# A decoder layer with a mixture-of-experts feed-forward: six experts' output products with tokens as columns, later GpSimd low parts, last norm on VectorE

## The chip, the cores and the metric

The kernel runs on one core of one Trainium2 chip. The metric is the device time of one execution in microseconds. A core has TensorE (PE; its weight loads are PEld), VectorE (DVE), ScalarE (ACT), GpSimd (POOL) and SyncE (SP), which here only issues DMAs. Each engine works through its own instructions in order; between engines the order is kept by semaphores alone. TensorE's clock has two levels here, 1.2 and 2.4 GHz, of which the chip grants one.

## The reference, cut to what matters

`x` is 16 x 512 x 256, in f32. One layer follows: an attention with its norm, a cross-attention with its norm, and the part that the change touches, a feed-forward of eight experts with a last norm:

```python
routing_weights = softmax(x @ router_w.T + router_b)            # tokens x 8
routing_mask = (w_flat > 0)
sorted_indices = argsort(-routing_mask, stable=True)[:capacity] # capacity = 1024 as the kernel uses it
inter = relu(einsum('ceh,ehi->cei', inputs_tokens, experts_inter))   # 256 -> 1024
out = einsum('cei,eih->ceh', inter, experts_out)                     # 1024 -> 256
out = out * inputs_weights[..., None]
combined = zeros_like(x_flat).at[used_tokens_indices].add(out)
x = layernorm(x + combined)
```

Every expert takes the first 1,024 tokens whose weight for it is above zero. When all weights are above zero, all eight experts take the same first 1,024 tokens, and all other rows only get the norm.

## The kernel before

`setup_and_attention` computes both attentions, tile by tile of 128 tokens, writes `x2` (the input of the feed-forward) to DRAM, and also writes the normed rows of all tokens to the output. `feed_forward` then handles groups of `CAP` = 1,024 tokens. After each group the number of groups is read from a register; with these inputs one group runs. Its accumulator `acc` holds the group's tokens, eight tiles (`GT`) of 128 tokens as partitions and 256 columns.

All matrix products run as `three_passes` (L134 to L139): each operand is kept as a high part in f32r and a low part (the rest), and TensorE adds high x high, low x high (or high x low) and the third combination into one PSUM bank, so one block of a product costs three matmuls.

For each expert (`expert(g, n, e, u)` in each engine's program; `u` is the one of two weight buffers in use):

- *First product* (`pe_tile`, L1576): for both halves `h` of 512 tokens and 8 chunks `i` of hidden columns, 6 matmuls with 512 columns (tokens) in one of four `up` banks. ScalarE writes the ReLU's high part `hT_hi` (L1489), VectorE the low part `hT_lo` and frees the bank (L1742). Hidden units lie on partitions, tokens are columns.
- *Output product* (L1655 to L1665): for each of 8 token tiles, 24 matmuls whose weights are 128 tokens of `hT` and whose 256 columns are the output channels of `w2`, in one of two `dn` banks. VectorE multiplies by the routing coefficient of the tokens (a column per partition) and adds into `acc` (L1755), which frees the bank.
- *Next weights*: SyncE loads `w1_raw` and `w2_raw` (one buffer each, 1 MB each, L86 and L87) once the low parts of the expert before are made. ScalarE makes the high parts (L1454, L1457) in four pieces at `i % 4 == 3` of the first product, GpSimd the low parts, one instruction of 128 x 2048 for each (L1518).

Expert 0 also makes the routing: logits, softmax, `chosen` (weight above zero), `ranks` by matmuls after the first output tile (L1664), and then on VectorE `coefficients` (L1725): steps 6 to 9 make `coef`, steps 10 to 12 the number of groups. The first six of expert 0's first products run in the last slots of the attention.

After each tile of expert 7 VectorE makes the statistics (L1760, L1762). For each pair of tiles GpSimd makes the scale and offset in four small instructions (L1542 to L1548), ScalarE applies them (L1509), and SyncE stores the pair (L1432).

## Time and profile before

| | us |
|---|---|
| median of 3 runs (lowest, highest) | 1288.14 (1287.87, 1289.94) |
| the profiled execution, its own time | 1288.03 |
| its span, first to last instruction | 1286.1 |
| TensorE busy | 1242.2 (97%) |
| VectorE busy | 876.0 (68%) |
| GpSimd busy | 632.1 (49%) |
| ScalarE busy | 574.5 (45%) |

The feed-forward takes about the last quarter of the span, from some 920 us on. Times in the rows are in microseconds from the span's start unless they are marked ns. A busy share is a mean over stages with different limits, so a stage has to be read by itself. TensorE's matmuls are pipelined, and their ends in the profile are modelled: the distance from start to start is what one costs. In a row in order of time, `[5.10 <-DVE acc L1755]` means that the engine sat idle for 5.10 us before it and what ended that.

### The profile page before, as it was taken

To read this page: it belongs to the slowest core of one execution; us is meant where nothing else is said; L and a number is where in the kernel's file an instruction comes from. 1 tells how busy PE (TensorE), PEld (TensorE's weight loads), DVE (VectorE), ACT (ScalarE), POOL (GpSimd) and SP (SyncE) were. 2 spreads that over 40 slices of the span, in tenths; PEclk is the share of its full clock that TensorE was granted. 3 is DMA by queue.
4 is the path that set the end of the run, shared out by engine and by line. 5 is a ranking of instruction groups with operands and counts; after the bars stand their busy time and mean duration, and the time that the engine had idled before them with its cause. 6 is when DMAs were issued, how large, how long until landed. Compare 5 with 4: busy or idle time off the path is not lost.

```text
span 1286.1 us, 22562 instructions
## 1 busy us (share of the span) xinstructions
PE 1242.2 (97%) x8080; PEld 1125.5 (88%) x8080; DVE 876.0 (68%) x1680; ACT 574.5 (45%) x1127; POOL 632.1 (49%) x994
## 2 busy tenths in 40 slices
PE   8968999999999999999999999988989999999997
PEld 7857999999999999999999999877788899899887
DVE  5536988888888889888888888887534323422433
ACT  2124546555565556465555655555514313421421
POOL 2225756757767567567577675664322112102201
PEclk9989999999999999999999999999989999999999
DMA  9831102111121111021111211320210112011001
GB/s 276 203 69 34 42 26 58 33 42 42 34 58 43 34 51 49 28 58 34 42 42 34 57 43 34 97 61 26 91 66 12 56 66 66 1 66 66 1 1 34
DMA packets 117458, 69.98 MB, mean 54 GB/s; under 512 B 74082, under 2 KB 114787, under 8 KB 117348
## 3 DMA queue, kind: packets, MB, share of 16 engines
q1 hardware_dynamic: 115316, 67.87, 18.0%
q8 instruction: 67, 1.10, 0.4%
q10 hardware_dynamic: 2032, 0.66, 0.2%
q14 instruction: 43, 0.35, 0.1%
HBM read 42.29 MB, written 26.22 MB: 53 GB/s over the span
## 4 chain that ended last, share of the span: by engine, by line
PE 86%; DVE 4%; POOL 2%; issue 1%; ACT 1%; POOLq 0%; DVEq 0%
PE ob L137 7%; PE ob L138 7%; PE ob L139 7%; PE sim L137 7%; PE sim L138 7%; PE sim L139 6%; PE pw L417 4%; PE pt L466 4%; PE pw L137 3%; PE pw L139 3%; PE pw L138 3%; PE pw L369 3%; PE pt L137 2%; PE pt L138 2%; PE pt L139 2%; PE pw L393 2%
## 5 line engine op out<-in xcount | busy, mean ns | idle before, releaser
L1518 POOL TENSOR_TENSOR w_lo<-w_raw,w_hi 128x2048 fp32r<-128x2048 f32 x16 | 73.6, 4605 | 230.8 <-ACT w_hi L1454 192.6
L137 PE MATMUL ob<-b_hi,pT_hi 128*128 128x256 f32 x512 | 153.2, 299 | 3.8 <-DVE pT_lo L822 3.8
L139 PE MATMUL ob<-b_hi,pT_lo 128*128 128x256 f32 x512 | 144.8, 283 | 0.0
L138 PE MATMUL ob<-b_lo,pT_hi 128*128 128x256 f32 x512 | 144.8, 283 | 0.0
L902 POOL TENSOR_TENSOR prob<-prob,rz 128x512 f32<-128x512 f32 x128 | 131.0, 1045 | 11.1 <-DVE rz L769 11.1
L684 ACT ACTIVATE prob<-prob 128x512 f32<-128x512 f32 x128 | 80.8, 631 | 112.7 <-DVE prob L815 111.9
L810 DVE TENSOR_REDUCE mx<-sim 128x8 f32<-128x512 f32 x128 | 87.9, 686 | 37.0 <-PE sim L139 35.7
L137 PEld LDWEIGHTS ob<-b_hi,pT_hi 128*128 128x128 f32 x512 | 97.5, 190 | 8.5 <-DVE pT_lo L822 7.8
L596 ACT ACTIVATE x<-h,nmr,rstd 128x256 f32<-128x256 f32 x128 | 76.2, 596 | 63.9 <-POOL nmr L836 59.1
L137 PE MATMUL sim<-a_hi,tT_hi 128*128 128x512 f32 x256 | 104.2, 407 | 0.0
L138 PE MATMUL sim<-a_lo,tT_hi 128*128 128x512 f32 x256 | 101.4, 396 | 0.0
L139 PE MATMUL sim<-a_hi,tT_lo 128*128 128x512 f32 x256 | 101.1, 395 | 0.0
L829 POOL TENSOR_SCALAR ve<-mv 128x1 f32<-128x1 f32 x128 | 28.0, 219 | 148.7 <-DVE mv L732 147.4
L138 PEld LDWEIGHTS ob<-b_lo,pT_hi 128*128 128x128 f32 x512 | 97.9, 191 | 0.7
L139 PEld LDWEIGHTS ob<-b_hi,pT_lo 128*128 128x128 f32 x512 | 97.7, 191 | 0.0
L1489 ACT ACTIVATE hT_hi<-zb 128x512 fp32r<-128x512 f32 x30 | 17.7, 591 | 168.1 <-PE zb L139 168.1
L815 DVE TENSOR_TENSOR prob<-sim,mx 128x512 f32<-128x512 f32 x128 | 88.3, 690 | 3.9
L690 ACT ACTIVATE pT_hi<-pt 128x512 fp32r<-128x512 f32 x128 | 75.9, 593 | 29.0 <-PE pt L466 29.0
L822 DVE TENSOR_TENSOR pT_lo<-pt,pT_hi 128x512 fp32r<-128x512 f32 x128 | 87.5, 684 | 1.2 <-ACT pT_hi L690 0.2
L466 PE MATMUL pt<-ident,prob 128*128 128x128 f32 x512 | 77.3, 273 | 3.5 <-DVE pT_lo L822 3.4
L765 DVE TENSOR_REDUCE zsum<-prob 128x16 f32<-128x1024 f32 x64 | 77.8, 1215 | 2.1
L137 PE MATMUL pt<-w_hi,hT_hi 128*128 128x256 f32 x256 | 73.0, 285 | 5.1 <-DVE acc L1755 5.1
(243 smaller groups left out, 3880.5 us busy)
## 6 DMA issues: line engine op xcount, KB each, us to landing
xraw<-in_x SPq DMA_DIRECT2D x16, 512.0 KB, 4.0
kv_scratch<-stage SPq DMA_DIRECT2D x32, 256.0 KB, 2.9
x_scratch<-x SPq DMA_DIRECT2D x64, 128.0 KB, 1.7
out_x<-o_sb SPq DMA_DIRECT2D x64, 128.0 KB, 1.7
w_raw<-in_L_ffn_experts_inter SPq DMA_DIRECT2D x8, 1024.0 KB, 5.0
w_raw<-in_L_ffn_experts_out SPq DMA_DIRECT2D x8, 1024.0 KB, 7.6
kraw<-kv_scratch SPq DMA_DIRECT2D x32, 128.0 KB, 3.0
vraw<-kv_scratch SPq DMA_DIRECT2D x32, 128.0 KB, 3.0
```

The source lines that it names most:

```text
L137: pe.matmul(out, lh, rh, start=first, stop=False)
L138: pe.matmul(out, lh, rl, start=False, stop=False)
L139: return pe.matmul(out, ll, rh, start=False, stop=last)
L466: last = pe.transpose(pt[:, r * P:(r + 1) * P], prob[:, par_n, c:c + P], ident[:, :])
L596: act.activation(dst, src, ACT.Identity, bias=nmr[:, q, ln:ln + 1], scale=rstd[:, q, ln:ln + 1]).then_inc(s[done], 1)
L684: act.activation(prob[:, q, h * HK:(h + 1) * HK], prob[:, q, h * HK:(h + 1) * HK], ACT.Exp).then_inc(s["exp_made"], 1)
L690: act.activation(pT_hi[:, h * 4:h * 4 + 4, :], pt[:, :].rearrange("p (r u) -> p r u", u=P), ACT.Copy).then_inc(s["pt_hi_made"], 1)
L765: dve.tensor_reduce(zsum[:, :], prob[:, q, :].rearrange("p (g j) -> p g j", j=NKV), AX.X, ALU.add).then_inc(s["sum_made"], 1)
L810: dve.tensor_reduce(mx[:, h * 8:h * 8 + 8], by_head(sim[h][:, :]), AX.X, ALU.max).then_inc(s["max_made"], 1)
L815: dve.tensor_tensor(by_head(prob[:, q, h * HK:(h + 1) * HK]), by_head(sim[h][:, :]), mx[:, h * 8:h * 8 + 8].unsqueeze(2).broadcast_to([P, ...
L822: dve.tensor_tensor(pT_lo[:, h * 4:h * 4 + 4, :], pt[:, :].rearrange("p (r u) -> p r u", u=P), f32(pT_hi[:, h * 4:h * 4 + 4, :]), ALU.subt ...
L902: pool.tensor_tensor(part, part, rz[:, q, h * 8:h * 8 + 8].unsqueeze(2).broadcast_to([P, 8, NKV]), ALU.mult).then_inc(s["p_ready"], 1)
```

## The change

1. *Output products of experts 1 to 6* (`across(e)`): 128 output channels of `w2` become the weights and 512 tokens of `hT` the columns, so that a bank holds 128 channels x 512 tokens, four banks of 24 matmuls per expert. The coefficient of a token now belongs to a column. VectorE multiplies the bank by `coef_all` (the expert's coefficients, the same on all partitions) into `part`, which frees the bank, and then copies (expert 1) or adds it into `accT`. Experts 0 and 7 stay as they were.
2. *Coefficients across*: after tile 4 of expert 0's output TensorE transposes `coef` (8 transposes), ScalarE copies the result to `coefT` (and waits for it ahead of its second pair of weight pieces for expert 1), SyncE stores it to `coef_scr` in DRAM and loads row `e` broadcast to 128 partitions, into two buffers by turns: for experts 1 and 2 at once, for `e + 2` once VectorE has freed the last output bank of expert `e`. These waits stand in SyncE's queue ahead of the next weights' loads.
3. *Back*: in expert 7, after each half of the first product, TensorE transposes half of `accT` (8 transposes, two banks), and VectorE adds each bank to `acc`.
4. *GpSimd's low parts for expert 1* wait for routing step 9 (`coef` is written).
5. *Last norm*: per tile, VectorE makes variance plus epsilon, GpSimd the power of -0.5, VectorE subtracts the mean and multiplies. ScalarE has no part in it. Stores: three of two tiles, then two of one tile.

```diff
@@ feed_forward
-    PART = 2
-    STORES = GT // PART
+    PARTS = [slice(0, 2), slice(2, 4), slice(4, 6), *(slice(i, i + 1) for i in range(6, GT))]
+    STORES = len(PARTS)
...
+    coefT = k.sb_over("t_sb", "coefT", [E, CAP], F32)
+    coef_all = [k.sb_at(f"coef_all{i}", [P, CAP], F32, k.offsets["woc"] + 4 * CAP * i) for i in range(2)]
+    accT = k.sb_over("x2", "accT", [P, MC, CAP], F32)
+    part = [k.sb_over("h1", "part0", [P, W], F32), k.sb_over("h2", "part1", [P, W], F32)]
...
+    DOWNS = 2 * GT + 4 * (E - 2)
+    def across(e):
+        return 0 < e < E - 1
+    def downs(g, e):
+        return DOWNS * g + (0 if e == 0 else GT + 4 * (e - 1))
@@ sp_program
+        def load_coefs(g, e):
+            if e > 2:
+                sp.wait_ge(s["dn_free"], downs(g, e - 1) + 2)
+            sp.dma_start(coef_all[e % 2][:, :], coef_scr[e:e + 1, :].broadcast_to([P, CAP])
+                         ).then_inc(s[f"coef_loaded{e % 2}"], 16)
         def expert(g, n, e, u):
+            if e < E - 1:
                 load_weights(n + 1, e + 1)
+            if is_first(e):
+                sp.wait_ge(s["coefT_copied"], g + 1)
+                sp.dma_start(coef_scr, coefT[:, :]).then_inc(s["coef_stored"], 16)
+                sp.wait_ge(s["coef_stored"], 16 * (g + 1))
+                load_coefs(g, 1)
+                load_coefs(g, 2)
+            if 0 < e < E - 3:
+                load_coefs(g, e + 2)
@@ act_program
             if is_first(e):
+                act.wait_ge(s["coefT_made"], g + 1)
+                for h in range(2):
+                    last = act.activation(coefT[:, h * W:(h + 1) * W], tr[h][0:E, :], ACT.Copy)
+                last.then_inc(s["coefT_copied"], 1)
                 act_weights(act, n + 1, e + 1, 1 - u, 2)
                 act_weights(act, n + 1, e + 1, 1 - u, 3)
@@ pool_program
         def expert(g, n, e, u):
+            if is_first(e):
+                pool.wait_ge(s["route_step"], g * STEPS + 9)
...
         def end(g):
+            for i in range(GT):
+                counted["ve"].wait_next(g * GT + i + 1)
+                pool.tensor_tensor(rstd[:, i:i + 1], ve[:, i:i + 1], half_exp[:, :], ALU.pow).then_inc(s["rstd_made"], 1)
@@ pe_program
+        def coefs_across(g):
+            pe.wait_ge(s["route_step"], g * STEPS + 9)
+            for i in range(GT):
+                last = pe.transpose(tr[i // HALF][0:E, i % HALF * P:(i % HALF + 1) * P], coef[:, i, :], ident[:, :])
+            last.then_inc(s["coefT_made"], 1)
+        def back(g, i):
+            if i == 0:
+                pe.wait_ge(s["accT_made"], 4 * (E - 2) * (g + 1))
+            if i >= 2:
+                pe.wait_ge(s["back_taken"], GT // 2 * g + i - 1)
+            for a in range(2):
+                for m in range(MC):
+                    last = pe.transpose(tr[i % 2][:, (a * MC + m) * P:(a * MC + m + 1) * P],
+                                        accT[:, m, (2 * i + a) * P:(2 * i + a + 1) * P], ident[:, :])
+            last.then_inc(s["back_made"], 1)
...
+                if e == E - 1:
+                    back(g, 2 * h)
+                    back(g, 2 * h + 1)
             pe.wait_ge(s["w_lo_made"], 2 * n + 2)
+            if across(e):
+                for i in range(4):
+                    h, c = i // 2, slice(i % 2 * P, (i % 2 + 1) * P)
+                    if i % 2 == 0:
+                        pe.wait_ge(s["up_free"], 4 + 2 * FC * n + (h + 1) * FC)
+                    pe.wait_ge(s["dn_free"], downs(g, e) + i + 1)
+                    for f in range(FC):
+                        last = three_passes(pe, dn[i % 2][:, :], (w2_hi[u][:, f, c], w2_lo[u][:, f, c]),
+                                            (h_of(hT_hi, h, f), h_of(hT_lo, h, f)), f == 0, f == FC - 1)
+                    last.then_inc(s["dn_made"], 1)
+                return
...
+                if is_first(e) and i == 4:
+                    coefs_across(g)
@@ dve_program
+            if across(e):
+                dve.wait_ge(s[f"coef_loaded{e % 2}"], 16 * ((E - 2) // 2 * g + (e + 1) // 2))
+                for i in range(4):
+                    h, m, done = i // 2, i % 2, 4 * (E - 2) * g + 4 * (e - 1) + i + 1
+                    c = slice(h * W, (h + 1) * W)
+                    dve.wait_ge(s["dn_made"], downs(g, e) + i + 1)
...
+                    dve.tensor_tensor(part[i % 2][:, :], dn[i % 2][:, :], coef_all[e % 2][:, c], ALU.mult
+                                      ).then_inc(s["dn_free"], 1)
...
+                        ins = dve.tensor_tensor(accT[:, m, c], accT[:, m, c], part[i % 2][:, :], ALU.add)
...
                     dve.bn_aggr(mv[:, i, :], bst[:, i, :]).then_inc(s["mv_made"], 1)
+                    counted["mv"].wait_next(GT * g + i + 1)
+                    dve.tensor_scalar(ve[:, i:i + 1], mv[:, i, 1:2], EPS, None, ALU.add).then_inc(s["ve_made"], 1)
+                    counted["rstd"].wait_next(GT * g + i + 1)
+                    dve.tensor_scalar(acc[:, i, :], acc[:, i, :], mv[:, i, 0:1], rstd[:, i:i + 1],
+                                      ALU.subtract, ALU.mult).then_inc(s["out_ready"], 1)
```

## Rows read from the trace of the kernel before

**Rows 1.** The page: busy us, share and instructions; the chain by engine.

```profile
PE 1242.2 (97%) x8080; PEld 1125.5 (88%) x8080; DVE 876.0 (68%) x1680; ACT 574.5 (45%) x1127; POOL 632.1 (49%) x994
PE 86%; DVE 4%; POOL 2%; issue 1%; ACT 1%; POOLq 0%; DVEq 0%
```

**Rows 2.** Order of time, TensorE, expert 1: start, us, engine, line, out<-in.

```profile
965.72 0.39 PE L137 MATMUL zb<-x2T_hi,w_hi 128*128 128x512 f32 x1
...
987.70 0.28 PE L137 MATMUL pt<-w_hi,hT_hi 128*128 128x256 f32 x1
...
1010.45 0.40 PE L137 MATMUL zb<-x2T_hi,w_hi 128*128 128x512 f32 x1
```

**Rows 3.** Order of time, TensorE, the output of expert 0.

```profile
945.97 0.58 PE L137 MATMUL pt<-w_hi,hT_hi 128*128 128x256 f32 x1 [5.10 <-DVE acc L1755]
...
951.69 0.28 PE L139 MATMUL ob<-w_hi,hT_lo 128*128 128x256 f32 x1
```

**Rows 4.** Order of time, VectorE and GpSimd, the routing chain of expert 0.

```profile
937.97 0.23 DVE L1728 TENSOR_TENSOR rank<-pw,taken_before 128x64 f32<-128x64 f32 x1 [2.61 <-PE pw L1634]
...
938.43 1.89 DVE L1730 TENSOR_SCALAR rank<-rank 128x64 f32<-128x64 f32 x1
940.35 4.44 DVE L1731 TENSOR_TENSOR coef<-rank,lg 128x64 f32<-128x64 f32 x1
...
945.02 0.15 DVE L1734 TENSOR_SCALAR groups_f<-fewest 128x1 f32<-128x1 f32 x1
945.31 0.15 DVE L1736 TENSOR_SCALAR groups_i<-groups_f 128x1 int32<-128x1 f32 x1
...
935.66 9.05 POOL L1518 TENSOR_TENSOR w_lo<-w_raw,w_hi 128x2048 fp32r<-128x2048 f32 x2 [11.51 <-ACT w_hi L1454]
```

**Rows 5.** Order of time, TensorE: transposes of 128 and of 8 columns.

```profile
879.21 0.60 PE L1566 MATMUL tr<-ident,acc 128*128 128x128 f32 x4
879.64 0.60 PE L1566 MATMUL zb<-ident,acc 128*128 128x128 f32 x4
...
926.27 0.66 PE L1623 MATMUL pw<-ident,lgT 8*128 8x8 f32 x8
```

**Rows 6.** DMA issues (count, KB, median us to landing); order of time, SyncE, ScalarE, VectorE.

```profile
w_raw<-in_L_ffn_experts_inter SPq DMA_DIRECT2D x7, 1024.0 KB, 5.0
w_raw<-in_L_ffn_experts_out SPq DMA_DIRECT2D x7, 1024.0 KB, 7.6
out_x<-acc SPq DMA_DIRECT2D x4, 256.0 KB, 2.2
...
out_x<-o_sb SPq DMA_DIRECT2D x7, 128.0 KB, 1.7
...
994.15 0.37 SPq L86 DMA_DIRECT2D w_raw<-in_L_ffn_experts_inter  x1
...
971.91 1.05 ACT L1454 ACTIVATE w_hi<-w_raw 128x1024 fp32r<-128x1024 f32 x1
...
973.48 0.69 DVE L1742 SCALAR_TENSOR_TENSOR hT_lo<-zb,hT_hi 128x512 fp32r<-128x512 f32 x1 [0.74 <-ACT hT_hi L1489]
```

**Rows 7.** Order of time, all engines, after the last matmul.

```profile
1279.14 0.48 DVE L1755 SCALAR_TENSOR_TENSOR acc<-ob,coef,acc 128x256 f32<-128x256 f32 x1 [1.60 <-PE ob L139]
...
1280.21 0.18 DVE L1762 BATCH_NORM_AGGREGATE mv_f<-bst_f 128x2 f32<-128x6 f32 x1
1280.57 0.22 POOL L1542 TENSOR_SCALAR ve_f<-mv_f 128x2 f32<-128x2 f32 x1 [4.02 <-DVE mv_f L1762]
...
1282.29 1.09 ACT L1509 ACTIVATE acc<-acc,nmr_f,rstd_f 128x256 f32<-128x256 f32 x2 [4.61 <-POOL nmr_f L1548]
```

**Rows 8.** Groups by line and form: busy us, mean ns, idle before.

```profile
L822 DVE TENSOR_TENSOR pT_lo<-pt,pT_hi 128x512 fp32r<-128x512 f32 x128 | 87.5, 684 | 1.2 <-ACT pT_hi L690 0.2
...
L1280 DVE TENSOR_SCALAR wog<-wo_raw,lng 128x256 f32<-128x256 f32 x1 | 0.4, 353 | 2.8 <-DMA lnb<-in_L_attn_ln_b 2.8
...
L833 POOL TENSOR_TENSOR rstd<-ve,epsc 128x1 f32<-128x1 f32 x128 | 72.0, 563 | 10.7
```

More of the change, by code:

```diff
@@ L1372, in feed_forward @@
     groups_i = small("groups_i", [P, 1], I32)
-    half_exp = small("half_exp", [P, PART])
+    half_exp = small("half_exp", [P, 1])
     bst = small("bst_f", [P, GT, 6])
@@ L1377, in feed_forward @@
     rstd = small("rstd_f", [P, GT])
-    nmr = small("nmr_f", [P, GT])
     s = {n: k.sem("f_" + n) for n in (
@@ L1423, in begin @@
             load_weights(g * E, 0)
+        def load_coefs(g, e):
[3 more added lines that the diff above has]
+                         ).then_inc(s[f"coef_loaded{e % 2}"], 16)
         def expert(g, n, e, u):
-            if not isinstance(e, int) or e < E - 1:
+            if e < E - 1:
                 load_weights(n + 1, e + 1)
+            if is_first(e):
[6 more added lines that the diff above has]
+                load_coefs(g, e + 2)
         def end(g):
-            for h in range(STORES):
-                sp.wait_ge(s["out_ready"], g * GT + (h + 1) * PART)
-                sp.dma_start(out_rows[bass.ds(g * CAP + h * PART * P, PART * P), :].rearrange("(i p) c -> p i c", p=P),
-                             acc[:, h * PART:(h + 1) * PART, :]).then_inc(s["out_stored"], 16)
+            for c in PARTS:
+                sp.wait_ge(s["out_ready"], g * GT + c.stop)
+                sp.dma_start(out_rows[bass.ds(g * CAP + c.start * P, (c.stop - c.start) * P), :].rearrange("(i p) c -> p i c", p=P),
+                             acc[:, c, :]).then_inc(s["out_stored"], 16)
             sp.reg_add(stores, stores, 16 * STORES)
@@ L1441, in sp_program, with act_weights @@
         sp.wait_ge(s["out_stored"], stores)
-    def act_weights(act, n, e, u, part):
+    def act_weights(act, n, e, u, part, g=0):
         if part == 0:
@@ L1505, in end @@
         def end(g):
[L1506 to L1510 removed]
+            pass
         groups_and_experts(act, "groups_act", begin, expert, end)
@@ L1751, in expert @@
                     coefficients(g)
+                if e == E - 1:
+                    for i in (2 * h, 2 * h + 1):
+                        dve.wait_ge(s["back_made"], GT // 2 * g + i + 1)
+                        dve.tensor_tensor(acc[:, 2 * i:2 * i + 2, :], tr[i % 2][:, :].rearrange("p (a c) -> p a c", a=2),
+                                          acc[:, 2 * i:2 * i + 2, :], ALU.add).then_inc(s["back_taken"], 1)
+            if across(e):
[4 more added lines that the diff above has]
+                    dve.wait_ge(s["dn_made"], downs(g, e) + i + 1)
+                    if e > 2 or i >= 2:
+                        dve.wait_ge(s["accT_made"], done - 2)
+                    dve.tensor_tensor(part[i % 2][:, :], dn[i % 2][:, :], coef_all[e % 2][:, c], ALU.mult
+                                      ).then_inc(s["dn_free"], 1)
+                    dve.wait_ge(s["dn_free"], downs(g, e) + i + 1 + 2)
+                    if e > 1:
+                        dve.wait_ge(s["accT_made"], done - 4)
+                        ins = dve.tensor_tensor(accT[:, m, c], accT[:, m, c], part[i % 2][:, :], ALU.add)
+                    else:
+                        ins = dve.tensor_copy(accT[:, m, c], part[i % 2][:, :])
+                    ins.then_inc(s["accT_made"], 1)
+                return
             for i in range(GT):
-                dve.wait_ge(s["dn_made"], GT * n + i + 1)
+                dve.wait_ge(s["dn_made"], downs(g, e) + i + 1)
                 col = coef[:, i, e:e + 1] if isinstance(e, int) else coef[:, i, bass.ds(e, 1)]
```

44 lines of the change are left out of this document (15 added, 29 removed).

## Prediction

> **What bounds the kernel now.** First the busy table: TensorE is busy 97% of the span, the next engine 68% [rows 1]. Second the chain that ended last: 86% of it is TensorE [rows 1], so a microsecond counts only if TensorE issues less, waits less, or if it falls after TensorE's last matmul. Third, TensorE's own order of time over one expert [rows 2]: expert 1's first product begins at 965.72, its output product at 987.70, expert 2 at 1010.45. So 96 matmuls of 512 columns took 21.98 us (229 ns each) and 192 of 256 columns took 22.75 us (118.5 ns each), with nothing idle between. Experts 1 to 7 all repeat this. Fourth, the one place in the feed-forward where TensorE stands still: expert 0's output products. TensorE waits 5.10 us for the first accumulate of VectorE [rows 3]. VectorE's routing chain [rows 4] shows why: the `is_le` on `rank` takes 1.89 us and the multiply into `coef` 4.44 us, on 64 elements, where a similar step reading PSUM, at 937.97, took 0.23. GpSimd ran two low parts back to back from 935.66 for 9.05 us [rows 4], 4.53 each: the first ends at about 940.2, where the `is_le` ends, the second at 944.7, where the multiply ends. VectorE stands still for as long as GpSimd's instruction lasts. The multiply has two SBUF inputs; the `is_le` has one, and immediates. Then TensorE resumes at half clock: from 945.97 to 951.69 it starts 26 matmuls [rows 3], 5.72 us against 26 x 0.1185 = 3.08.
>
> The sums below are against the profiled execution (1288.03 us, span 1286.1); the runs' median, 1288.14, is 0.1 above it, which I add once at the end. About 0.2% (2.6 us) is what a measurement of this kernel can tell from no change.
>
> **Output products with tokens as columns.** Experts 1 to 6 issue 4 x 24 matmuls of 512 columns in place of 8 x 24 of 256. These have the form of the first products (changing 128x128 weights, 512 moving columns, f32r), so I take 229 ns: 96 x 0.229 = 21.98 against 22.75. That is 0.77 per expert, **6 x 0.77 = -4.6**. Bounds: -4.6, and 0 if two half-width matmuls cost what one wide one does. The Trainium skill (TensorE: Matmul & The Clock Gate, Back-to-back issue gap) gives an isolated gap of N/2.4 + 2.5 ns; by it the fusion saves only 2.5 ns a pair, an estimate of 1.4 us over six experts. The rows' own spacing for both widths decides here.
>
> **GpSimd's later low parts.** GpSimd now waits for routing step 9 (`coef`) before the low parts of expert 1. Then the `is_le` from 938.43 and the multiply take about 0.23 each, so `coef` is ready near 938.9. The reduction `fewest` and then `groups_f` and `groups_i`, 128x1 tensor-scalars on SBUF, follow [rows 4]. GpSimd starts 0.18 after a VectorE end (1280.39 to 1280.57 in [rows 7]), near 939.1, before `groups_f`, which starts 0.23 after the multiply ended (944.79 to 945.02). So two small operations still meet GpSimd's 4.5 us. In the likeliest case they don't stop: then the first accumulate is done by about 940.1 and TensorE, which needs the bank at 940.9, doesn't wait. That takes back 5.10 and the clock's 5.72 - 3.08 = 2.64: **-7.7**. No row shows a 128x1 VectorE operation beside a GpSimd one; the nearest that ran unhindered is the one that reads PSUM (0.23), the nearest that stopped is the 64-element `is_le`. I take the first, since the two that stopped both ran over 64 elements, but by little (rival B). With the clock kept and the wait gone expert 1 starts near 959, so w1's low part, now over near 943.7, still comes 15 us early.
>
> **Coefficients across.** Eight transposes on TensorE after tile 4 of expert 0. Four of 128 columns follow four at a distance of 0.43 [rows 5], so eight take 0.86; eight small ones took 0.66 with the last one's own length [rows 5]. With 0.1 for changing form: **+1.0** (0.6 to 1.2). Then ScalarE makes two copies, and only then its two w2 high parts for expert 1, queued behind its new wait. Expert 1 starts at 965.72 - 7.7 + 1.0 = 959.0; tiles 5 to 7 (2.84 each) lie between, so the transposes end at 950.5. Copies taken at the 1.05 of a high part (twice their size) [rows 6] end at 952.6, the high parts at 954.7, GpSimd's low part at 959.3, for an output product at 981. Free. SyncE's loads for expert 2 wait for the same low part: issued at 959.3, w1 lands 5.0 later, 964.3; ScalarE wants it 6.19 after the stage starts (971.91 - 965.72, [rows 2, 6]), 965.2. Free too, by 0.9. Ahead of them on SyncE's queue are the coefficients' store and two broadcasts, from about 953; a store takes 1.7 and a MB 5.0 [rows 6], so they are in flight or over by then.
>
> **The broadcasts of later experts.** From expert 1 to 4, SyncE waits until VectorE has freed the last output bank of expert e, then loads the coefficients of e+2 (512 KB), and only then the weights of e+2. Before, those were issued at 994.15, 6.4 us into expert 1's output [rows 6], as GpSimd's low part ended. Now: the next expert starts at U; VectorE's last multiply runs from U+0.2 to U+0.9 (0.68, the 512-element form of [rows 8]); the broadcast goes out at about U+1.0 and, an issue taking 0.37, w1 at U+1.4. Landing takes 5.0, plus the 512 KB ahead of it. The second MB lands 2.6 later than the first, each from its own issue, or 3.0 with that issue, so half a MB costs 1.5: U+7.9. ScalarE wants w1 at U+6.19 and would stand 1.7. But TensorE is four banks ahead: VectorE frees tile 4's bank at 973.48 + 0.69 [rows 6], which is U+8.45, and tile 8 starts at U + 8 x 1.374 = U+10.99. Slack 2.5. **0**, with 0.8 to spare; bounds 0 and +1 for each of the four.
>
> **VectorE per output product.** Eight accumulates of 0.48 become four multiplies from PSUM (0.68) and four adds (under 0.7) in 22 us: hidden. The adds read SBUF twice, so they could stop behind GpSimd's w2 low part. That ended just before the load at 994.15 [rows 6]; the first add would come 24 x 0.229 + 0.9 = 6.4 after 987.70, at 994.1. The bank is freed by the multiply, so even a stop costs TensorE nothing.
>
> **Back.** Sixteen transposes in the last expert, twice eight: 2 x (0.86 + 0.1) = **+1.9** (1.3 to 2.4). VectorE's four additions (0.68) go between its splits, before each of which it idles 0.74 [rows 6].
>
> **The last norm.** Before, from the last accumulate at T = 1279.14: statistics done at T+1.25, then three hops and four operations on GpSimd, two of ScalarE's, end of span at T+6.96; the last ScalarE operation ends at T+4.24 [rows 7]. After: variance plus epsilon 0.15 at T+1.37, power on GpSimd 0.18 later for 0.56 (128x1 [rows 8]) to T+2.26, the final VectorE operation 0.35 (its form with a per-partition scalar [rows 8]) to T+2.65. From there the same 2.72 to the end, less 2.2 - 1.7 = 0.5 since the last store is 128 KB instead of 256 [rows 6]: T+4.87. **-2.1** (-1.6 if the smaller store gains nothing). VectorE now needs 2.65 per tile and TensorE gives it one in 2.84: it keeps up, but by 0.2 only; 0.1 more than 2.84 would cost 0.7 at the end.
>
> **Sum:** -4.6 - 7.7 + 1.0 + 0 + 1.9 - 2.1 = -11.5. 1288.03 - 11.5 = 1276.5, and on the median's level **1276.6**.
>
> **Rivals.**
> B. The 128x1 operations do stop behind GpSimd. For it: `is_le`, also one input with immediates, stopped; against it: only its length. GpSimd's low part ends at 939.1 + 4.53 = 943.65; from `groups_f`'s start to TensorE's resumption took 945.97 - 945.02 = 0.95, so TensorE resumes at 944.6, idle for 3.7 us, and if the clock falls again it loses 2.6 more. 1276.6 + 6.3 = **1282.9** (1280.3 if the clock holds). The Trainium skill (SBUF — State Buffer, Who interferes with whom) says that a VectorE instruction in a two-port mode or with two SBUF inputs contends with GpSimd and the later one blocks fully, that reductions never do, and Vector Engine (DVE) Microarchitecture Reference, Performance modes, that the two-port mode engages for an even outermost count, or an odd one equal in source and destination. A count of 1 is equal in both, so by the letter B happens. The trace agrees for the two stretched steps and is silent on one element.
> C, slower. The weights land late at four experts: landing at U+L, TensorE stands L - 8.7 at tile 8 each time. To eat 11.5 the four must lose 2.9 each, w1 landing at U+11.6, 10 us after its issue, where the longest row is 7.6 [rows 6]. At 12 us after issue, U+13.4: 4 x 4.7 = 18.8 less 11.5, **1295**; a wait that long also lowered the clock in [rows 3].
> D. Wide output products save nothing: 1276.6 + 4.6 = **1281.2**.
>
> **Chances.** Forecast 0.50, B 0.35, D 0.05, C 0.05, mixtures of smaller misses near no change 0.05. Faster by over 0.2% (under 1285.6): 0.88; within: 0.07; slower: 0.05. The range takes in B with its lowered clock and 1.4 us of small waits, and below the forecast the cheap ends of the transposes (0.4 + 0.6) and half a microsecond: 1275.0 to 1284.3. The forecast's own is 1275.0 to 1278.6.
>
> **What the profile after should show.** `rank` and `coef` near 0.2 us; `groups_f` 0.15 (forecast) or about 4.5 (B); TensorE's wait in expert 0 gone or 3.7. Output products of experts 1 to 6 in 21.98 us. The loads of w1 issued 1.4 after an expert starts, ScalarE's first high part about 1.7 later than U+6.2, TensorE with no wait at tile 8. End of span 4.9 after the last accumulate. I am wrong if wide products are not at 229 ns, if a wait shows at tile 8, or if VectorE falls behind in the last eight tiles.

## The result and the profile after

The changed kernel takes 1279.54 us (median of 4 runs, 1278.65 to 1280.85), the kernel before, on the same chip, 1288.93 (1287.87 to 1289.94): a ratio of 0.9928, 95% interval [0.9911, 0.9945]. The forecast was 1276.6 in a range of 1275.0 to 1284.3. The profiled execution took 1279.84 us, its span is 1278.1. One of ten executions of `before_all_64`, an experiment below, took 1763.75 us at a mean granted clock of 0.653, and its ratio is taken without it.

The page of the kernel after: busy us, share and instructions (of before: [rows 1]).

```profile
PE 1240.2 (97%) x7528; PEld 1096.3 (86%) x7528; DVE 885.4 (69%) x1700; ACT 570.7 (45%) x1121; POOL 632.3 (49%) x986
```

552 matmuls fewer (576 less from the fusion, 24 transposes more), 8.0 us less span, but only 2.0 us less busy time: what went away is mostly waiting. The order of time of the kernel after says where. First expert 0 (of before: [rows 3, 4]); the columns are start, us, engine, line, operation, out<-in, and in brackets the idle time before and who ended it.

```profile
939.78 0.23 DVE L1786 TENSOR_TENSOR rank<-pw,taken_before 128x64 f32<-128x64 f32 x1 [2.61 <-PE pw L1657]
...
940.24 0.20 DVE L1788 TENSOR_SCALAR rank<-rank 128x64 f32<-128x64 f32 x1
940.47 0.23 DVE L1789 TENSOR_TENSOR coef<-rank,lg 128x64 f32<-128x64 f32 x1
...
940.92 0.16 DVE L1792 TENSOR_SCALAR groups_f<-fewest 128x1 f32<-128x1 f32 x1
941.21 0.16 DVE L1794 TENSOR_SCALAR groups_i<-groups_f 128x1 int32<-128x1 f32 x1
...
940.88 4.60 POOL L1548 TENSOR_TENSOR w_lo<-w_raw,w_hi 128x2048 fp32r<-128x2048 f32 x1 [14.92 <-DVE fewest L1791]
955.17 4.61 POOL L1548 TENSOR_TENSOR w_lo<-w_raw,w_hi 128x2048 fp32r<-128x2048 f32 x1 [9.69 <-ACT w_hi L1487]
...
951.07 1.03 PE L1665 MATMUL pw<-ident,coef 128*8 128x128 f32 x8
951.86 0.37 PE L138 MATMUL ob<-w_hi,hT_hi 128*128 128x256 f32 x1
```

The `is_le` at 940.24 takes 0.20 where it took 1.89, the multiply into `coef` 0.23 where it took 4.44. GpSimd's low part runs from 940.88 to 945.48, and the two 128x1 operations at 940.92 and 941.21 run inside it in 0.16 each: rival B did not happen. TensorE has no wait in expert 0's output products. The eight transposes at 951.07 push the next product 0.79 back. Also, GpSimd's second low part no longer follows the first: it comes at 955.17, because ScalarE now makes w2's high parts only after the coefficients.

Next, TensorE in experts 1 to 7 of the kernel after, at the borders of the stages (of before: [rows 2]), and the last expert's transposes.

```profile
960.37 0.39 PE L138 MATMUL zb<-x2T_hi,w_hi 128*128 128x512 f32 x1
...
982.36 0.39 PE L138 MATMUL pt<-hT_hi,w_hi 128*128 128x512 f32 x1
...
1004.68 0.39 PE L138 MATMUL zb<-x2T_hi,w_hi 128*128 128x512 f32 x1
...
1026.66 0.39 PE L138 MATMUL pt<-hT_hi,w_hi 128*128 128x512 f32 x1
...
1049.04 0.39 PE L138 MATMUL zb<-x2T_hi,w_hi 128*128 128x512 f32 x1
...
1226.35 0.39 PE L138 MATMUL zb<-x2T_hi,w_hi 128*128 128x512 f32 x1
...
1237.34 1.03 PE L1676 MATMUL pw<-ident,accT 128*128 128x128 f32 x8
```

A first-product stage is 21.99 (960.37 to 982.36), as before. The output stage of expert 1 is 22.32 (982.36 to 1004.68), that of expert 2 22.38 (1026.66 to 1049.04), and so on in turn: 232.5 and 233.1 ns a product, not 229.0.

The late weights, expert 2 of the kernel after (U = 1004.68, its first product's start): SyncE's issue of w1, ScalarE's first high part, VectorE freeing the bank of tile 4; then, from the page, the median landing of w1's loads (count, KB each, us).

```profile
1006.20 0.37 SPq L87 DMA_DIRECT2D w_raw<-in_L_ffn_experts_inter  x1
...
1013.05 1.06 ACT L1484 ACTIVATE w_hi<-w_raw 128x1024 fp32r<-128x1024 f32 x1 [2.07 <-DMA w_raw<-in_L_ffn_experts_inter]
...
1014.62 0.69 DVE L1800 SCALAR_TENSOR_TENSOR hT_lo<-zb,hT_hi 128x512 fp32r<-128x512 f32 x1 [2.93 <-ACT hT_hi L1519]
...
w_raw<-in_L_ffn_experts_inter SPq DMA_DIRECT2D x8, 1024.0 KB, 6.5
```

w1 goes out at U+1.52, ScalarE starts on it at U+8.37 after standing 2.07, and VectorE has freed tile 4's bank at 1014.62 + 0.69 = U+10.63. TensorE needs it at U+10.99 and never waits. It was closer than forecast: the slack left is 0.36 us, and 0.78, 0.45 and 0.58 in experts 3 to 5 (the same VectorE end at U+10.21, 10.54 and 10.41).

The tail, kernel after (of before: [rows 7]).

```profile
1273.01 0.48 DVE L1836 SCALAR_TENSOR_TENSOR acc<-ob,coef,acc 128x256 f32<-128x256 f32 x1
...
1274.70 0.55 POOL L1573 TENSOR_TENSOR rstd_f<-ve_f,half_exp 128x1 f32<-128x1 f32 x1 [2.30 <-DVE ve_f L1845]
1275.38 0.41 DVE L1847 TENSOR_SCALAR acc<-acc,mv_f,rstd_f 128x256 f32<-128x256 f32 x1 [0.83 <-POOL rstd_f L1573]
```

The end of the span comes 5.09 after the last accumulate, where it came 6.96 after it.

Cutting both profiled executions at the same events gives the account of the change. The cuts are VectorE's first routing step (937.97 before [rows 4], 939.78 after), the first products of experts 1 and 7 (965.72 [rows 2] and 1234.22; 960.37 and 1226.35), the last accumulate (1279.14 [rows 7]; 1273.01) and the end of the span.

| stretch | before | after | difference | forecast |
|---|---|---|---|---|
| start to the routing step | 937.97 | 939.78 | +1.8 | 0 |
| routing step to expert 1 | 27.75 | 20.59 | -7.2 | -6.7 |
| experts 1 to 6 | 268.50 | 265.98 | -2.5 | -4.6 |
| expert 7 to the last accumulate | 44.92 | 46.66 | +1.7 | +1.9 |
| to the end of the span | 6.96 | 5.09 | -1.9 | -2.1 |
| span | 1286.1 | 1278.1 | -8.0 | -11.5 |

The first line holds a difference in the attention and its set-up, whose instructions the change leaves alone. Part of it is the clock. The window from 60 to 110 us, first of before, then of after, shows it; after the window stand its length, the busy times of PE, PEld, DVE, ACT and POOL, and then the granted clock, the DMA share and GB/s.

```profile
60.00:110.00 50.00, 35.43 (x187) 29.65 (x185) 21.55 (x45) 16.03 (x36) 16.07 (x37) 0.90 0.27 61
```

```profile
60.00:110.00 50.00, 35.44 (x179) 29.45 (x178) 20.92 (x45) 14.26 (x34) 14.52 (x35) 0.83 0.28 64
```

The mean granted clock was 0.90 in one execution and 0.83 in the other: of 50 us, 10 and 17 were at 1.2 GHz. From 110 to 880 the granted clock is 1.00 in both. Of the 1.8 us, 0.7 are there before this window (TensorE's 201st matmul starts at 45.87 and 46.56) and 1.1 arise in it. The feed-forward shows -9.8, the medians -9.4, and the profiled pair's -8.0 holds these 1.8 us. Whether the change has a share in them isn't shown. They vary between executions, but not evenly: VectorE's first routing step starts at 935.70 to 939.14 in the four profiled kernels that are the one before or grow out of it, and at 938.62 to 941.95 in the ten that are the changed kernel or grow out of it. For this reason the experiments below are read from the routing step to the end of the span, "the feed-forward": 348.13 before, 338.32 after.

### The profile page after: what moved, and what is told of

It reads as the page before. It is cut to its first block, busy times and chain, and to the rows that moved or that the text cites. A ratio compares the mean times of both kernels' runs of the same rounds, so it can differ in the third digit from the quotient of the medians.

```text
span 1278.1 us, 21498 instructions
## 1 busy us (share of the span) xinstructions
PE 1240.2 (97%) x7528; PEld 1096.3 (86%) x7528; DVE 885.4 (69%) x1700; ACT 570.7 (45%) x1121; POOL 632.3 (49%) x986
## 4 chain that ended last, share of the span: by engine, by line
PE 87%; DVE 4%; POOL 1%; issue 1%; ACT 1%; POOLq 0%; DVEq 0%
PE ob L138 7%; PE ob L140 7%; PE ob L139 7%; PE sim L138 7%; PE sim L139 7%; PE sim L140 7%; PE pw L418 4%; PE pt L467 4%; PE pw L138 3%; PE pw L139 3%; PE pw L140 3%; PE pw L370 3%; PE pt L140 2%; PE pt L138 2%; PE pt L139 2%; PE pw L394 2%
## 5 line engine op out<-in xcount | busy, mean ns | idle before, releaser
L834 POOL TENSOR_TENSOR rstd<-ve,epsc 128x1 f32<-128x1 f32 x128 | 72.1, 563 | 10.7
```

## The experiments

**GpSimd's wait alone.** The kernel before with that one wait:

```diff
         def expert(g, n, e, u):
+            if is_first(e):
+                pool.wait_ge(s["route_step"], g * STEPS + 9)
```

> The kernel before with GpSimd's wait for routing step 9 alone. Here both low parts follow back to back after the wait. If 128x1 operations on VectorE don't stop behind GpSimd: -7.9 us against before, 1281.0, TensorE's wait in expert 0 gone, clock at 2.4 GHz throughout the stage. If they do: -1.5 at most.

Measured: 1280.51 us (1280.26 to 1281.29) against 1288.21, ratio 0.9937 [0.9921, 0.9954]. VectorE's routing steps, then GpSimd, then TensorE's first product of expert 1, order of time of this kernel:

```profile
939.14 0.23 DVE L1730 TENSOR_TENSOR rank<-pw,taken_before 128x64 f32<-128x64 f32 x1 [2.61 <-PE pw L1636]
...
939.61 0.20 DVE L1732 TENSOR_SCALAR rank<-rank 128x64 f32<-128x64 f32 x1
...
940.25 9.15 POOL L1518 TENSOR_TENSOR w_lo<-w_raw,w_hi 128x2048 fp32r<-128x2048 f32 x2 [14.94 <-DVE fewest L1735]
...
958.99 0.39 PE L137 MATMUL zb<-x2T_hi,w_hi 128*128 128x512 f32 x1
```

From the routing step to expert 1 it takes 958.99 - 939.14 = 19.85 us in place of 27.75: -7.9, where the prediction had -7.7. The whole feed-forward takes 340.26, which is 7.9 less too. The step stands, its parts (the wait and the clock) included: no stretch at 1.2 GHz follows.

**The changed kernel without GpSimd's wait.** The same two lines taken out of the changed kernel.

```diff
-            if is_first(e):
-                pool.wait_ge(s["route_step"], g * STEPS + 9)
```

> The changed kernel without GpSimd's wait for routing step 9; all else as changed. Theory (the wait took away VectorE's two stretched steps, TensorE's wait and the fall of its clock): is_le and coef stretched again to some 6 us together, TensorE waits about 5 us in expert 0 and runs some 5 us at 1.2 GHz; 7 to 8 us slower than the changed kernel, 1286.5 to 1287.5. Rival (the stretched steps went for another reason, such as the delayed w2 parts): GpSimd's first low part alone stretches only is_le by about 1.7 us, TensorE waits 1 us or less, at most 2 us slower. In the changed kernel the w2 high parts come after the coefficients, so a mixture is to be had: is_le stretched to the end of the w1 part (1.9), coef short, TensorE's wait gone.

Measured: 1280.27 us (1279.89 to 1280.98), ratio 0.9938 [0.9921, 0.9954]: within 0.8 us of the changed kernel, which the medians can't tell apart. The trace can. Its VectorE, GpSimd and TensorE in expert 0:

```profile
939.16 1.86 DVE L1786 TENSOR_SCALAR rank<-rank 128x64 f32<-128x64 f32 x1
941.06 0.23 DVE L1787 TENSOR_TENSOR coef<-rank,lg 128x64 f32<-128x64 f32 x1
...
936.39 4.58 POOL L1548 TENSOR_TENSOR w_lo<-w_raw,w_hi 128x2048 fp32r<-128x2048 f32 x1 [11.52 <-ACT w_hi L1484]
955.22 4.61 POOL L1548 TENSOR_TENSOR w_lo<-w_raw,w_hi 128x2048 fp32r<-128x2048 f32 x1 [14.24 <-ACT w_hi L1487]
...
942.47 0.38 PE L138 MATMUL pt<-w_hi,hT_hi 128*128 128x256 f32 x1 [0.86 <-DVE acc L1834]
```

The `is_le` is stretched as before, until GpSimd's first low part ends at 940.97. But the multiply behind it takes 0.23, because the second low part isn't there: it waits for ScalarE's w2 high parts, which the change has put behind the coefficients' transposes, and starts at 955.22. TensorE waits 0.86 instead of 5.10, the clock stays, and the feed-forward takes 339.49, 1.2 more than after. So two parts of the change each remove most of the same 7.9 us (ScalarE's new wait was not run in the kernel before by itself; the trace shows what it does here). Alone, the wait is worth 7.9; with the other in place it is worth 1.2. The prediction credited all of it to the wait.

**Two elements in place of one.** A tensor-scalar over 128x2 goes in before `groups_f`; its result isn't used.

```diff
+            dve.tensor_scalar(probe[:, :], taken_before[:, 0:2], float(CAP), None, ALU.is_lt)
             dve.tensor_scalar(groups_f[:, :], ...
```

> The changed kernel with one more VectorE operation ahead of groups_f: a tensor-scalar of 128x2 from SBUF to a scratch tile, about 0.04 us after GpSimd's low part begins. If two elements are enough to stop behind GpSimd where one isn't: this operation lasts 4.4 to 4.6 us, the first accumulate comes near 945.6, TensorE waits 3.5 to 3.8 us, its clock perhaps falls (2.6 more). If small operations pass whatever their count is, it lasts 0.16 and nothing else changes.

Measured, in one execution: 1286.77 us. VectorE, GpSimd and TensorE, order of time, and below them the window of TensorE's slow stretch (columns as above):

```profile
941.34 4.52 DVE L1793 TENSOR_SCALAR probe_f<-taken_before 128x2 f32<-128x2 f32 x1
...
941.30 4.54 POOL L1549 TENSOR_TENSOR w_lo<-w_raw,w_hi 128x2048 fp32r<-128x2048 f32 x1 [14.92 <-DVE fewest L1792]
...
946.71 0.58 PE L138 MATMUL pt<-w_hi,hT_hi 128*128 128x256 f32 x1 [3.62 <-DVE acc L1838]
...
946.60:953.50 6.90, 6.79 (x35) 6.79 (x36) 0.94 (x3) 0.00 (x0) 0.00 (x0) 0.56 0.01 2
```

Two elements stop for the whole of GpSimd's instruction (4.52 against 4.54); one element, in the changed kernel, does not (0.16). The operations differ in more than the count: the added one has one arithmetic step and f32 output, `groups_f` two steps and f32, `groups_i` one step and int32. As both of those pass, the count is the likely cause, but no run has the very same operation over one element. The price is that of rival B: TensorE idles 3.62 (3.7 was worked out), the clock falls to 1.2 GHz behind it, and the feed-forward takes 344.90, 6.6 more than after (6.3 was worked out). B's sum was right; only its condition was not met.

**More ahead of the weights.** Another 512 KB broadcast is put on SyncE's queue ahead of the weights of experts 3 to 6.

```diff
             sp.dma_start(coef_all[e % 2][:, :], ...
+            if e > 2:
+                sp.dma_start(extra[:, :], coef_scr[e:e + 1, :].broadcast_to([P, CAP])).then_inc(s["extra_loaded"], 16)
```

> The changed kernel with one more broadcast of 512 KB ahead of the weights of experts 3 to 6. In the changed kernel ScalarE starts the first high part 8.4 us after the expert starts (U), TensorE doesn't wait. By the slack of the prediction (part at U+8.65 at the latest) another 1.3 to 1.5 us makes it U+9.7 to 9.9, and TensorE stands 1.0 to 1.3 us at tile 8 of experts 2 to 5: 4 to 5 us in all. If the slack was undersized, as the next banks could hide it too: no wait.

Measured, in one execution: 1286.8 us. SyncE's issue of w1 (behind the added broadcast), ScalarE's first high part, and TensorE at both ends of expert 2's first products:

```profile
1008.83 0.38 SPq L87 DMA_DIRECT2D w_raw<-in_L_ffn_experts_inter  x1
...
1016.51 1.06 ACT L1487 ACTIVATE w_hi<-w_raw 128x1024 fp32r<-128x1024 f32 x1 [3.36 <-DMA w_raw<-in_L_ffn_experts_inter]
...
1006.86 0.39 PE L138 MATMUL zb<-x2T_hi,w_hi 128*128 128x512 f32 x1
...
1029.92 0.39 PE L138 MATMUL pt<-hT_hi,w_hi 128*128 128x512 f32 x1
```

ScalarE starts at U+9.65, 1.28 later than in the changed kernel, and the stage grows from 21.99 to 23.06 (1006.86 to 1029.92); the four stages are 23.07, 23.08, 23.26 and 23.27, together 4.8 us, and the feed-forward takes 343.15 for 338.32: +4.8. 1.28 of delay less 0.36 of slack is 0.92 and the stage lost 1.07, so the deadline is within 0.2 of where the rows put it. Rival C's mechanism is real. The change stays 0.36 us clear of it in the profiled execution.

**The last norm alone.** The kernel before with the change's norm: variance and final operation on VectorE, the power alone on GpSimd, tile by tile, and single stores for the last two tiles.

```diff
-                act.wait_ge(s["nmr_made"], STORES * g + h + 1)
...
-                    act.activation(acc[:, i, :], acc[:, i, :], ACT.Identity, bias=nmr[:, i:i + 1],
...
+                    counted["rstd"].wait_next(GT * g + i + 1)
+                    dve.tensor_scalar(acc[:, i, :], acc[:, i, :], mv[:, i, 0:1], rstd[:, i:i + 1],
+                                      ALU.subtract, ALU.mult).then_inc(s["out_ready"], 1)
```

> The kernel before with the change's last layer norm (eps, subtract and multiply on VectorE tile by tile, GpSimd's power alone, five stores with single ones for the last two tiles) and nothing else. My prediction priced this at -2.1 us; in the changed kernel the stretch from the last accumulate to the end of the span is 5.09 us instead of 6.96, so -1.87. My theory: the pieces add, the tail measures 5.0 to 5.2 us and the median lies 1.7 to 2.1 us under the kernel before. Rival: with the narrow output products of experts 0 to 6 nothing else changes for the tail either, but expert 7's VectorE work per tile (now 2.8 us) holds TensorE back at the output banks; then the stretch from expert 7's first output product to the last accumulate is over 22.9 us and the gain is under 1.5 us.

Measured: 1285.98 us (1284.79 to 1286.47) against 1288.48, ratio 0.9979 [0.9969, 0.9988]. Its last accumulate is at 1279.64 in a span of 1284.8: a tail of 5.16, -1.8. From the first to the last start, expert 7's output products take 22.62 us in it and 22.63 in before, so VectorE does not hold TensorE. The feed-forward takes 346.47, -1.7.

Four runs of one execution each then took up the miss, the output stages that took 22.3 to 22.4 us instead of 21.98; their stages are read from the trace.

**What moves: x2T.** The wide output products of experts 1 to 6 read x2T as their moving operand instead of the hidden layer, so the output is another.

```diff
-                            (h_of(hT_hi, h, f), h_of(hT_lo, h, f)), f == 0, f == FC - 1)
+                            (x2T_hi[:, f % 2, h * W:(h + 1) * W], x2T_lo[:, f % 2, h * W:(h + 1) * W]),
+                            f == 0, f == FC - 1)
```

> The wide output products of experts 1 to 6 take their moving operand from x2T (the one of the first products, two chunks used again and again) in place of hT; the weights stay w2, so the output products are not the layer's. Changed kernel: 22.35 us per output stage (96 matmuls at 232.8 ns), first products 21.98 (229.0 ns). If the moving operand, its place or its content, makes the difference: 21.98 us. If the weights or the length of the accumulation do: 22.35 still.

Measured: TensorE at both ends of the output stages of experts 1 and 2.

```profile
982.33 0.39 PE L138 MATMUL pt<-x2T_hi,w_hi 128*128 128x512 f32 x1
...
1004.73 0.39 PE L138 MATMUL zb<-x2T_hi,w_hi 128*128 128x512 f32 x1
...
1026.70 0.39 PE L138 MATMUL pt<-x2T_hi,w_hi 128*128 128x512 f32 x1
...
1048.68 0.39 PE L138 MATMUL zb<-x2T_hi,w_hi 128*128 128x512 f32 x1
```

22.40 in experts 1, 3 and 5, 21.98 in 2, 4 and 6. The same instructions over the same x2T: the two differ only in which of the two sets of weight buffers they read.

**What stands: w1.** The wide output products take their weights from w1's buffers and still move the hidden layer; the output is another.

```diff
-                        last = three_passes(pe, dn[i % 2][:, :], (w2_hi[u][:, f, c], w2_lo[u][:, f, c]),
+                        wc = slice((4 * (i % 2) + f // 2) * P, (4 * (i % 2) + f // 2 + 1) * P)
+                        last = three_passes(pe, dn[i % 2][:, :], (w1_hi[u][:, f % 2, wc], w1_lo[u][:, f % 2, wc]),
```

> The wide output products take their weights from w1 (the one of the first products) in place of w2; the moving operand stays hT, so the output products are not the layer's. If the weights make the difference: 21.98 us per output stage. If the moving operand or the length of the accumulation does: 22.35.

Measured: 22.38 us in all six stages. Weights that go at 229 ns in the first products go at 233 under the hidden layer. Neither operand alone is the cause.

**Another order of the passes.** High weights by low, high by high, low by high.

> The three passes of a wide output product in another order: high weights x low columns, high x high, low weights x high columns. The same sum. If the spacing hangs on which columns stream (in the first products the pass of the low weights is the short one, 226 ns, the two of the high weights are 231 and 230): the spacings change places, the stage stays at 22.3 to 22.4. If streaming the same columns in two successive passes is what is cheap: the high x high and low x high passes now follow each other and the stage falls by 96 x 2 to 4 ns, to 22.0 to 22.2.

Measured: 22.27 and 22.35 us by turns, 0.05 and 0.03 less, 0.24 in all six. Not the cause.

**Accumulation restarted.** The wide products start a new sum every six matmuls, as the first products do, instead of every 24; three quarters of the sum are lost.

```diff
-                                            (h_of(hT_hi, h, f), h_of(hT_lo, h, f)), f == 0, f == FC - 1)
+                                            (h_of(hT_hi, h, f), h_of(hT_lo, h, f)), f % 2 == 0, f % 2 == 1)
```

> The wide output products start a new accumulation every six matmuls, as the first products do, so only the last six of 24 stay in the bank (part of the sum is left out). If the length of the accumulation, that is adding to what is in the bank, makes the difference: 21.98 us per stage. If an operand does: 22.35.

Measured: 22.32 and 22.38 us by turns, unchanged. Not the cause.

These four leave where the operands lie as the next thing to try. The byte at which each begins in its partition follows from the sizes of the tiles declared before it, and several tiles with 257 columns shift those behind them by 32. So the last three runs change addresses only.

**Six buffers moved by 32 bytes.**

```diff
-    ... k.sb_over("x1", "w2_lo1", [P, FC, C])]
+    ... k.sb_at("w2_lo1", [P, FC, C], F32R, k.offsets["x1"] + 32)]
+    # hT_hi of wqx, wox_hi, tT_hi, tT_lo: by 0, -32, 32, 32; hT_lo of qT_hi, wox_lo, b_hi, b_lo: by 32, -32, 0, 0
```

> The changed kernel with six buffers moved by 32 bytes, so that every operand of the output products (the low output weights of every second expert, five of the eight tiles of the hidden layer) begins at a multiple of 64 bytes. Left as it is: everything else. In the changed kernel a wide output stage takes 22.32 or 22.39 us where a first-product stage of the same 96 products of 512 columns takes 21.98; with x2T as the moving operand (a_move_x) the experts with one set of weight buffers took 21.97 and those with the other, whose low part begins 32 bytes off, 22.40. Theory A: what costs 4 ns a product is an operand that begins at an odd multiple of 32 bytes; then all six output stages fall to 21.97 to 22.05 us and the kernel gains 6 x 0.38 = 2.2 us. Rival B: it is how the addresses of the two operands stand to each other, whatever their multiple; then some stages change in either direction, none by more than 0.45, and they aren't all alike. Rival C: the buffers' addresses have nothing to do with it: 22.32 and 22.39 stay.

Measured: 1278.24 us (1276.76 to 1278.68), ratio 0.9918 [0.9902, 0.9935]. TensorE at the ends of the stages of experts 1 and 2 of this kernel, and at the first product of expert 7:

```profile
962.14 0.39 PE L138 MATMUL zb<-x2T_hi,w_hi 128*128 128x512 f32 x1
...
984.13 0.39 PE L138 MATMUL pt<-hT_hi,w_hi 128*128 128x512 f32 x1
...
1005.91 0.40 PE L138 MATMUL zb<-x2T_hi,w_hi 128*128 128x512 f32 x1
...
1027.92 0.39 PE L138 MATMUL pt<-hT_hi,w_hi 128*128 128x512 f32 x1
...
1049.70 0.40 PE L138 MATMUL zb<-x2T_hi,w_hi 128*128 128x512 f32 x1
...
1224.85 0.40 PE L138 MATMUL zb<-x2T_hi,w_hi 128*128 128x512 f32 x1
```

The output stage takes 21.78 us (984.13 to 1005.91, 1027.92 to 1049.70), in all six experts; in experts 2, 4 and 6 only the hidden layer's buffers moved. That is 226.9 ns a product, less than the first products' 229. Experts 1 to 6 take 262.71 for 265.98, -3.3; the narrow products of experts 0 and 7, which read the same buffers the other way round, take 0.3 longer each. The feed-forward takes 335.77, 2.6 less than the changed kernel's. The medians do not separate the two kernels (ratios 0.9918 and 0.9928, with overlapping intervals); the trace does. So the addresses make the difference. The stages fell further than theory A had it (21.97 to 22.05), and by more than the 0.45 that rival B allowed. The next two runs try theory A's rule:

**Every large tile at a multiple of 64 bytes, after and before.** Five small tiles are declared elsewhere so that all large ones fall on multiples of 64.

```diff
     wqx = k.sb("wqx", [P, PAIRS, C + 1])
+    bq = k.sb("bq", [P, MC])
     xraw = k.sb("xraw", [P, 2, TPB, C + 1])
+    bvsum = k.sb("bvsum", [P, 2, MC])
     x1 = k.sb("x1", [P, 2, TPB, C + 1])
+    ve = k.sb("ve", [P, 2, 4])
```

> The changed kernel with five small tiles declared at other places, so that every large tile of both parts begins at a multiple of 64 bytes, where 21 of them began at an odd multiple of 32; no instruction differs but in its addresses. With six buffers moved (multiples_of_64) the wide output stages fell from 22.32 and 22.39 to 21.78 us, 6 ns a product. Theory A: any matmul that reads a moved operand gains. In the feed-forward the first products, whose low moving operand was off by 32, go from 21.98 to 21.78 (7 x 0.2 = 1.4 us more), the output stages stay 21.78, the narrow output stages of experts 0 and 7 lose 0.2 to 0.6 each. The attention's products, which fill 850 of the first 940 us, read their operands at such addresses too: if they lose 1 to 2.5 per cent, 8 to 20 us more, so 1255 to 1269 us. Rival: the attention's products, of 128 to 257 columns and with rows of 1028 bytes among their operands, or held by other engines, gain nothing: 1275 to 1277 us.

> The kernel before with the same five small tiles declared at other places, nothing else. It tells what the fusion of two products of 256 columns into one of 512 is worth where both are placed alike. Before, a narrow output stage is 22.74 or 22.79 us (192 products, 118.5 ns each) against 22.32 or 22.39 for the wide one. My theory of the missing gain: the prediction took the wide product from the first products (229.0 ns), whose operands lie better, and the narrow one from badly placed operands; placed alike, narrow products go to 116 to 117.5 ns (22.3 to 22.55 us) against 21.78, so fusing is worth 0.5 to 0.8 us a stage, not 0.40. Rival: narrow products are not slowed by the addresses (their stage stays at 22.74); then fusing is worth 0.96 a stage when placed well. In the attention what after_all_64 gains is gained here as well, by the same amount within 1 us.

Measured, in the changed kernel: 1280.34 us (1279.34 to 1280.63), ratio 0.9941 [0.9925, 0.9958]. In the kernel before: 1287.51 us, ratio 0.9997 [0.9987, 1.0007], no difference. TensorE at the ends of expert 1's stages, first the changed kernel so placed, then the kernel before so placed:

```profile
959.12 0.39 PE L138 MATMUL zb<-x2T_hi,w_hi 128*128 128x512 f32 x1
...
981.38 0.39 PE L138 MATMUL pt<-hT_hi,w_hi 128*128 128x512 f32 x1
...
1003.71 0.40 PE L138 MATMUL zb<-x2T_hi,w_hi 128*128 128x512 f32 x1
```

```profile
963.41 0.40 PE L137 MATMUL zb<-x2T_hi,w_hi 128*128 128x512 f32 x1
...
985.69 0.28 PE L137 MATMUL pt<-w_hi,hT_hi 128*128 128x256 f32 x1
...
1008.19 0.39 PE L137 MATMUL zb<-x2T_hi,w_hi 128*128 128x512 f32 x1
```

Theory A falls, and 1280.34 lies above its 1255 to 1269 as well as above its rival's 1275 to 1277. The wide output stage is back at 22.33, and the first products, whose operands are now all at multiples of 64, went up from 21.99 to 22.26 (22.28 and 22.29 in the later experts). In the kernel before the narrow output stage fell from 22.75 [rows 2] to 22.50 and the first products rose to 22.28. The attention didn't gain the 8 to 20 us that I allowed: I had carried one stage's 6 ns over to all matmuls without a row that says so.

Set against the remainder by 128 of each operand's first byte the stages read like this (moving high and low, weights high and low; a slash parts the buffers of one operand). The remainders are worked out from the declared sizes, taking the first tile to begin at a multiple of 128, which no run shows; ns are stage / 96:

```
first products, after                    x2T 0, 32              w1 0, 0      229.0
a_move_x, experts 2, 4, 6                x2T 0, 32              w2 0, 0      228.9
a_move_x, experts 1, 3, 5                x2T 0, 32              w2 0, 96     233.3
wide outputs, after, experts 2, 4, 6     hT 0, 96 / 32, 32 / 96, 0   w2 0, 0      233.1
wide outputs, after, experts 1, 3, 5     hT 0, 96 / 32, 32 / 96, 0   w2 0, 96     232.5
b_weights_w1, all wide outputs           hT 0, 96 / 32, 32 / 96, 0   w1 0, 0      233.1
multiples_of_64, all wide outputs        hT 0, 0                w2 0, 0      226.9
after_all_64, first products             x2T 64, 0              w1 0, 0 / 64, 64   231.9 to 232.2
after_all_64, wide outputs               hT 0, 0 / 64, 64 / 0, 64   w2 64, 0 / 64, 64   232.4 to 232.6
```

The only stages below 228 ns are those in which all four operands begin at a multiple of 128 bytes, as they happened to do in the run named for multiples of 64. Those with one low part off by 32 cost 2 ns more, the others 5 to 6. More operands off do not add up: with w2's low part off as well, the wide outputs take 232.5 and not 233.1. That is a reading after the fact: no run of its own put every operand at a multiple of 128, and how the two operands' remainders act together stays open.

## Why the prediction was right, and what it mis-sized

The range held and the time is 2.9 us above the point. Of this, 0.8 is the level: the kernel before ran at 1288.93 beside the changed one, 1288.14 in the runs that the forecast stood on. The other 2.1 is the difference between -11.5 and the medians' -9.4. Its steps are compared with the feed-forward of the profiled pair, which shows -9.8:

- **Wide output products: the term that was mis-sized.** Forecast -4.6, measured -2.5. I took 229 ns from the first products because the form is the same. The rows were right and the transfer wasn't: same form, other buffers. The products ran at 232.5 and 233.1 ns, and with six buffers moved by 32 bytes at 226.9. The bounds (-4.6 to 0) held it as built, but with the six buffers moved experts 1 to 6 take 262.71 - 268.50 = -5.8, beyond the lower one; that is fusion and addresses together. Of the rule from the Trainium skill (TensorE: Matmul & The Clock Gate, Back-to-back issue gap) the trace agrees with neither the gap (215.8 ns by it, 226.9 at the least here) nor quite with the saving: 1.4 us by it, 2.5 measured. It was nearer than my 4.6; the measured saving of 4.2 ns a pair (22.75 - 22.35 over 96) depends on the addresses: placed on multiples of 64 on both sides it is 22.50 - 22.33 = 0.17 us in expert 1, 1.8 ns a pair, and 22.60 - 22.31 = 0.29 us in expert 2, 3.0 ns.
- **GpSimd's later low parts: right in size, wrong in credit.** -7.7 forecast, -7.9 measured, with the clock kept. The wait brings it alone, but so, for all but 1.2 us, does ScalarE's new wait, which takes the second low part out of the way. The prediction traced that delay (GpSimd's low part after 954.7; it came at 955.17) and didn't count what it does to the routing chain.
- **One element doesn't stop.** The choice between forecast and rival B, 0.50 to 0.35, was the open question; no row decided it, and it fell to the forecast. I took the Trainium skill's rule (Vector Engine (DVE) Microarchitecture Reference, Performance modes, with SBUF — State Buffer, Who interferes with whom) to say that a count of 1 stops. That was misread: the page puts its condition on the outermost dimension that is larger than 1, and a single element has none, so by its letter the two-port mode is not promised there. The trace has one element at 0.16 us, and agrees with the rule at two elements with 4.52.
- **Coefficients across and back.** 0.79 in place of 1.0 and 1.7 in place of 1.9: eight transposes cost 0.79 each time. In expert 0 nothing came on top for the change of form. In expert 7 twice 0.79 is 1.58, and the rest lies around them: the second half of the first product took 11.08 for 10.99, the output stage 23.01 for 22.94 to the last accumulate.
- **Late weights.** 0 forecast, 0 measured. The issue at U+1.52 for U+1.4 and the landing 6.5 after it where the estimate's 7.9 - 1.4 was the same 6.5. The deadline came as the slack of 2.5 said: ScalarE stood 2.07 and 0.36 was left, where I had 0.8.
- **The last norm.** -2.1 forecast, -1.9 and -1.8 measured in two kernels. The final VectorE operation takes 0.41, not the 0.35 of the row that I took, and comes 0.13 after GpSimd's end (1275.25 to 1275.38) where I had put 0.04: it ends at T+2.78 and not T+2.65. VectorE keeps up with TensorE, but just: 2.78 of 2.84 per tile.

What the change's two halves come to is seen only in this sum: the fusion's -2.5 is spent on its own transposes, +0.8 and +1.7. Output products summed transposed are worth nothing here as placed, and some 2.7 us together with the moved buffers (-5.8, +2.5 and twice 0.3, all from traces); the gain of the change is that of the routing stretch and of the norm, 7.9 and 1.9.

## What to carry to other kernels

When a stall has two possible removers in one change, ask of each what is left if the other is there: the chain that makes a late operand later can take a contender out of the way as a wait does. A duration transfers from one matmul stage to another only with its form and its addresses: before fusing products for a few ns each, see where the operands begin, since in the traces moving six buffers by 32 bytes was worth as much (2.6 us) as the fusion (2.5). And read a late transfer by its deadline: a 2 us stand of ScalarE cost nothing, 1.3 us more cost four stages a microsecond each.

## What the runs showed of the hardware

- A VectorE tensor-scalar over 128x1 in f32 SBUF ran in 0.16 us inside a GpSimd instruction of 4.60 us with two SBUF inputs; one over 128x2 took 4.52 and ended with it. I had not expected the border between one and two.
- Back-to-back matmuls of 128x128 weights by 512 columns, f32r, ran at 226.9, 229.0 and 232 to 233 ns. The wide output products went from 232.5 and 233.1 to 226.9 with six buffers moved by 32 bytes and no other edit, in all six experts, and the first products from 229.0 to about 232 with other tiles moved.
- An idle of 0.86 us of TensorE (the changed kernel without GpSimd's wait) left the clock at 2.4 GHz; one of 3.62 was followed by a stretch of 6.9 us with a mean granted clock of 0.56.
